# A two-layer graph network on one core: sorted rows laid out for one load per four pairs, tables found part by part, second pass without a loop

## The reference, cut to what matters

```python
# layer 0
agg = segment_sum(x[dst], src)            # row = src, col = dst
agg = agg / (deg[:, None] + 1e-6)
x = layernorm(x + relu(concatenate([x, agg]) @ W + b))
# layer 1 (4 heads of 32)
s = leaky_relu(x_l[src] + x_r[dst] + (edge_attr @ W_e))
alpha = softmax of einsum(s, att) over the edges of each dst
x = layernorm(x + segment_sum(x_l[src] * alpha, dst) + bias)
```

## Time and profile before

| | us |
|---|---|
| median of 3 runs | 1609.33 |
| lowest and highest | 1607.97, 1613.49 |
| the profiled execution | 1610.33 |
| its span, first to last instruction | 1608.5 |
| mean granted TensorE clock | 0.896 of full speed |

### The profile page before, as it was taken

How to read it: one execution, slowest core, us unless ns; L and a number is a source line. 1 busy time by engine, 2 the same in 40 slices (tenths; PEclk the granted TensorE clock), 3 DMA queues, 4 the chain that set the end, 5 groups by cost and what they waited for, 6 DMA issues and landing times. The chain is left out here.

```text
span 1608.5 us, 35020 instructions
## 1 busy us (share of the span) xinstructions
PE 1221.8 (76%) x8692; PEld 1083.7 (67%) x8702; DVE 1002.4 (62%) x2116; ACT 771.1 (48%) x2046; POOL 970.2 (60%) x970
## 2 busy tenths in 40 slices
PE   4887866888887778776797787888878887878650
PEld 2685856877777667765564777777777877777640
DVE  5333324644554444455654588888888878888858
ACT  0375644444455545410144665665655656556311
POOL 3277777777677766740001777777777777777501
PEclk9999889998999998988998899998999989999855
DMA  2233335555555555544101433333333333332001
GB/s 67 73 114 93 105 106 151 140 145 147 144 145 148 150 140 149 149 113 109 40 12 55 134 97 96 95 97 88 95 92 92 96 91 90 87 93 83 26 1 40
DMA packets 235701, 160.30 MB, mean 100 GB/s; under 512 B 29816, under 2 KB 220622, under 8 KB 235580
## 3 DMA queue, kind: packets, MB, share of 16 engines
q1 hardware_dynamic: 206396, 100.85, 24.1%
q0 software_dynamic: 29184, 58.01, 11.9%
HBM read 127.10 MB, written 34.39 MB: 100 GB/s over the span
## 5 line engine op out<-in xcount | busy, mean ns | idle before, releaser
L390 POOL DMA_INDIRECT sorted_rows<-row,place_idx x456 | 468.8, 1028 | 230.8 <-issue 173.5
L1134 POOL DMA_INDIRECT xl<-xl_rows,index_c x456 | 468.8, 1028 | 158.0 <-issue 132.5
L428 ACT COPY onehot_t<-ps_t 128x500 f32<-128x500 f32 x114 | 65.6, 575 | 284.2 <-PE ps_t L735 274.9
L1410 PE MATMUL ps_cs<-w_e,attr_t 128*125 128x128 f32 x912 | 193.9, 298 | 3.7 <-DVE work_c L1324 3.1
L1411 PE MATMUL ps_cs<-src_sum,onehot_ct 128*125 x912 | 191.3, 295 | 0.0
L601 DVE TENSOR_TENSOR away_s<-row_in,pair_bucket 128x4 f32<-128x4 f32 x135 | 21.9, 162 | 223.3 <-DMA row_in<-sorted_rows 215.9
L1410 PEld LDWEIGHTS ps_cs<-w_e,attr_t 128*125 128x125 f32 x912 | 155.4, 213 | 4.2 <-issue 3.3
L746 PE MATMUL ps_g<-row_in,onehot_s 128*128 128x129 f32 x976 | 143.9, 295 | 18.2 <-DVE onehot_s L606 18.2
L1411 PEld LDWEIGHTS ps_cs<-src_sum,onehot_ct 128*125 128x125 f32 x912 | 153.2, 210 | 0.0
L746 PEld LDWEIGHTS ps_g<-row_in,onehot_s 128*128 128x128 f32 x976 | 131.9, 210 | 24.6 <-issue 22.5
L1148 ACT ACTIVATE apart<-column,dst_lo 125x128 f32<-125x128 f32 x456 | 145.6, 394 | 4.6 <-PEq L858 4.6
(11 more groups left out here) (307 smaller groups left out, 2385.8 us busy)
## 6 DMA issues: line engine op xcount, KB each, us to landing
row_in<-sorted_rows SPq DMA_DIRECT2D x540, 66.0 KB
attr<-in_ea SPq DMA_DIRECT2D x456, 62.5 KB
attr_c<-in_ea SPq DMA_DIRECT2D x456, 62.5 KB
sorted_rows<-row,place_idx POOLq DMA_INDIRECT x456
xl<-xl_rows,index_c POOLq DMA_INDIRECT x456, 3.3
xl_rows<-x_nodes SPq DMA_DIRECT2D x5, 320.0 KB, 2.5
out<-x SPq DMA_DIRECT2D x4, 320.0 KB
sorted_rows<-x SPq DMA_DIRECT2D x5, 66.0 KB, 2.0
```

Source lines behind the costliest of these rows:

```text
L390: pool.indirect_dma_start(out=m.sorted_rows.rearrange("k p w -> (k p) w"), out_offset=bass.IndirectOffsetOnAxis(ap=m.place_idx[:, k:k + 1] ...
L1134: pool.indirect_dma_start(out=xl[x][:, u, :], out_offset=None, in_=m.xl_rows, in_offset=bass.IndirectOffsetOnAxis(ap=index[half][:, b * U ...
L1410: pe.matmul(out, attr_t[off % 2][:, u, :], m.w_e[:], start=True, stop=False)
```

## The change

1. `sorted_rows` is laid out as (128, tiles, row) instead of (tiles, 128, row). Four table tiles that follow each other lie side by side in each partition's stretch, so one transfer of 128 x 2112 bytes loads them. `tile2_i` has the first tile of each pair block, and a new table `offset2_i` says which of the four each pair uses; TensorE, VectorE and ScalarE load those numbers.
2. VectorE makes the one-hot matrix of a pair block with four operations of 128 columns, straight from `row_in`. In the last part every second pair block (from 109 on) has it made by ScalarE.
3. `find_ends(p)` finds dst and src of the slots of one part only, in a step of its own; `by_slot` skips the parts of `pick` that are zero. Places are split in two numbers (place mod 128, place / 128). The setup's order changes: places of part 0 come before the number tables.
4. The flags of the softmax move from step 14 to step 78.
5. In `attend` the loop is gone, and POOL reads the indices from `src_idx` itself.

The core of the diff:

```diff
             def load_rows(q):
...
-                tiles = numbers(nc, sp, m.tile2_i, q * U, U, NP * T2 - 1)
-                for u in range(U):
-                    sp.dma_start(row_in[q % B2][:, u, :], m.sorted_rows[bass.ds(tiles[u], 1), :, :].rearrange(
-                        "o p w -> (o p) w")).then_inc(row_back[q % B2], 16)
+                tile = numbers(nc, sp, m.tile2_i, q, 1, NP * T2 - U)[0]
+                sp.dma_start(row_in[q % B2][:], m.sorted_rows[:, bass.ds(tile, U), :]).then_inc(row_back[q % B2], 16)
...
+        def by_scalar(q):
+            return q >= FIRST_ODD and (q - FIRST_ODD) % 2 == 0        # FIRST_ODD = (NP - 1) * G2 + 1
...
+            def make_onehot_s(q):                                      # ScalarE
+                act.wait_ge(row_back[q % B2], 16 * (q // B2 + 1))
...
+                for u in range(U):
+                    act.activation(shift_s[:, u:u + 1], row_in[q % B2][:, bass.ds(offsets[q][u], 1), P + 1], ACT.Identity,
+                                   bias=m.bucket2[:, k:k + 1], scale=-1.0).then_inc(shift_ready, 1)
+                for u in range(U):
+                    act.activation(apart_s[:, u, :], m.column[:], ACT.Abs, bias=shift_s[:, u:u + 1]).then_inc(
+                        apart_s_ready, 1)
+                act.wait_ge(src_summed, q - RINGS + 1)
+                act.activation(onehot_s[q % RINGS][:], apart_s[:], ACT.Relu, bias=1.0, scale=-1.0).then_inc(onehot_s_odd, 1)
...
             def make_onehot_s(q):                                      # VectorE
-                dve.tensor_tensor(away[:], row_in[q % B2][:, :, P + 1], m.bucket2[:, q * U:(q + 1) * U],
-                                  ALU.subtract).then_inc(away_found, 1)
-                dve.tensor_tensor(onehot_s[q % RINGS][:], repeat(m.column[:], 1, U), repeat(away[:], 2, P),
-                                  ALU.is_equal).then_inc(onehot_s_ready, 1)
+                for u in range(U):
+                    src = row_in[q % B2][:, bass.ds(offsets[q][u], 1), P + 1]
+                    dve.scalar_tensor_tensor(onehot_s[q % RINGS][:, u, :], m.column[:], m.bucket2[:, k:k + 1],
+                                             src.broadcast_to([P, P]), ALU.add, ALU.is_equal).then_inc(onehot_s_ready, 1)
...
+            def find_ends(p):                                          # TensorE
+                for at, table in ((0, dst_f), (128, src_f)):
+                    out = ps_c[0:TE, at:at + n]
+                    if p:
+                        pe.matmul(out, table[:, p - 1], pick[:, p - 1, cols], start=True, stop=False)
+                    mm = pe.matmul(out, table[:, p], pick[:, p, cols], start=(p == 0), stop=True)
...
             find_counts(0)
-            by_slot(ps_a[:, 2:4, :].rearrange("p a w -> p (a w)"), TE, dst_f).then_inc(dst_found, 1)
-            turn_starts(0)
+            find_ends(0)
             for c in range(5):
-                if c == 4:
-                    pe.wait_ge(numbers_ready, 1)
+                if c == 3:
+                    pe.wait_ge(dst_ready, 1)
                 sum_chunk(0, c, CHUNK_BANKS[c])
-            count_pairs(0)
-            by_slot(ps_g[:, 2:4, :].rearrange("p a w -> p (a w)"), TE, src_f).then_inc(src_found, 1)
             turn_places(0)
             pick_places(0)
+            turn_starts(0)
+            count_pairs(0)
...
                 for q in gathers(j):                                   # VectorE
-                    make_onehot_s(q)
+                    if not by_scalar(q):
+                        if q % 3 == 0 or q >= FIRST_ODD:
+                            n = 1 if q >= FIRST_ODD - 1 else 3
+                            found = numbers(nc, dve, m.offset2_i, q * U, n * U, U - 1)
...
+                        found = numbers(nc, pe, m.offset2_i, q * U, 3 * U, U - 1)      # TensorE, with window2_i
...
-        FIRST_AT = 14
+        FIRST_AT = 78
...
# attend
-            for j in range(static):
-                one_step(0, j)
-            with engine.Fori(0, LOOPS) as i:
-                for s in range(RING):
-                    one_step(i, static + s)
-            for j in range(static + LOOPS * RING, NB + LAG + 2):
+            for j in range(NB + LAG + 2):
                 one_step(0, j)
...
-                    pool.tensor_copy(index[half][0:TE, :], m.src_idx[:, bass.ds(j * U, GS)]).then_inc(index_ready, 1)
-                    pool.wait_ge(index_ready, i * 2 + off // B + 1)
```

More of the change, by code:

```diff
@@ L453, in _ @@
                         row_copied, 1)
+                if j + 2 < NB:
+                    act.wait_ge(dst_ready, min(((j + 2) * U + U - 1) // CR, NP - 1) + 1)
+                    make_onehot(j + 2)
+                for q in gathers(j):
+                    if by_scalar(q):
+                        act.wait_ge(pairs_ready, NP)
+                        offsets[q] = numbers(nc, act, m.offset2_i, q * U, U, U - 1)
+                        make_onehot_s(q)
                 if (p := phase_at.get((j, "totals"))) is not None:
@@ L557, in _ @@
             link(dve.tensor_tensor(t_of[:], iota_k[0:1, :], node_of[0:1, :], ALU.subtract))
[L558 to L561, removed]
+            find_ends(0)
+            for c in range(5):
+                place_chunk(0, c, CHUNK_BANKS[c])
+            dve.wait_ge(preset, PRESET)
+            place_window(0)
             find_first_pairs(0)
@@ L639, in _ @@
                 if (p := phase_at.get((j, "placed"))) is not None:
+                    find_ends(p)
+                if (p := phase_at.get((j, "stored"))) is not None:
                     place_window(p)
@@ L699, in pick_places, with find_ends @@
                 pe.matmul(out, place_t[:, p % 2, :], pick[:, p, cols], start=(p == 0), stop=True).then_inc(window_found, 1)
-            def by_slot(bank, rows, table):
-                for c in range(CC):
-                    mm = pe.matmul(bank[0:rows, 0:K], table[:, c], pick[:, c, :], start=(c == 0), stop=(c == CC - 1))
+            def find_ends(p):
+                cols = windows[p]
+                n = cols.stop - cols.start
+                if p:
+                    pe.wait_ge(chunk_placed, 5 * (p + 1))
+                for at, table in ((0, dst_f), (128, src_f)):
+                    out = ps_c[0:TE, at:at + n]
+                    if p:
+                        pe.matmul(out, table[:, p - 1], pick[:, p - 1, cols], start=True, stop=False)
+                    mm = pe.matmul(out, table[:, p], pick[:, p, cols], start=(p == 0), stop=True)
+                mm.then_inc(ends_of_slot, 1)
+            def by_slot(bank, rows, table):
+                for p in range(NP):
+                    cols = windows[p]
+                    out = bank[0:rows, cols]
+                    if p:
+                        pe.matmul(out, table[:, p - 1], pick[:, p - 1, cols], start=True, stop=False)
+                    mm = pe.matmul(out, table[:, p], pick[:, p, cols], start=(p == 0), stop=True)
                 return mm
@@ L800, in _ @@
                 if (p := phase_at.get((j, "window"))) is not None:
+                    find_ends(p)
+                if (p := phase_at.get((j, "picked"))) is not None:
                     pick_places(p)
@@ L809, in _ @@
                         pe.wait_ge((first_copied, ends_copied)[which], 1)
-                        for c in range(CC):
-                            mm = pe.matmul(ps_p[0:4, 0:K], ends4[:, which, c, :], pick[:, c, :],
-                                           start=(c == 0), stop=(c == CC - 1))
-                        mm.then_inc(ends_found, 1)
+                        by_slot(ps_p, 4, ends4[:, which]).then_inc(ends_found, 1)
 def center(vec, done, y, stats):
@@ L1032, in attend @@
         xl = [sb(f"xl{b}", [P, U, P]) for b in range(RING)]
-        index = [sb(f"index_c{b}", [P, GS], I32) for b in range(2)]
         onehot = [sb(f"onehot_c{b}", [TE, U, P]) for b in range(RING)]
@@ L1088, in attend, with steps @@
         block = ctx.enter_context(nc.Block())
-        def steps(engine, one_step, static=STATIC):
-            for j in range(static):
-                one_step(0, j)
-            with engine.Fori(0, LOOPS) as i:
-                for s in range(RING):
-                    one_step(i, static + s)
-            for j in range(static + LOOPS * RING, NB + LAG + 2):
+        def steps(engine, one_step):
+            for j in range(NB + LAG + 2):
                 one_step(0, j)
@@ L1115, in _ @@
         def _(pool):
-            for half in range(2):
-                pool.memset(index[half][:], 0).then_inc(index_preset, 1)
-            pool.wait_ge(index_preset, 2)
             def one_step(i, off):
@@ L1452, in one_step @@
                         turned_back, 1)
-            steps(pe, one_step, STATIC - 1)
+            steps(pe, one_step)
 def finish(nc, g, m, out):
```

169 lines of the change are left out of this document (99 added, 70 removed).

## The result

The changed kernel takes 1603.3 us (median of 20 runs, 1595.9 to 1613.7) against 1613.3 us of the kernel before in the same number of runs: a ratio of 0.9941, 95% interval 0.9927 to 0.9954. It is 0.6% faster where 4.5% was forecast, and 1603 lies outside the range of 1505 to 1582. The spans of these two are 1604.5 us after and 1608.5 before: they lie 4 us apart where the medians lie 10 apart. One of the four runs of the experiment with four row loads took 5090 us, and the time given there is the median of the other three.

What follows compares the result with a forecast made beforehand. POOL's floor (5.33 us a block) was taken to bound the first 44 store blocks, SyncE's queue the next 70 and the tail. Savings of 9 + 3 + 24 + 14.5 + 22 = 72.5 us gave 1537 us, range 1518 to 1558.

Steps and rivals of the forecast that it cites:

- the first 44 blocks: First 176 row stores, 237.5 us: POOL's floor sets the pace, 5.40 to 5.33 us a block, 3 us saved.
- Rival 3: Store stage and tail: register loads form a chain that nothing covers, 6.45 us a block, 1651 us in all; chance 0.05.
- SyncE's queue as the bound of the last 70 blocks: Last 280 row stores: one row load for four takes blocks from 5.85 to 5.5 us, 24 us saved.
- My 5.36 for TensorE: Last 70 store blocks: TensorE's sum of 4.86 + 0.3 + 0.2 us a block, taken as 5.5 with VectorE's latency.
- rival 1: Whole kernel: nothing but POOL's floor binds, 104 us saved, 1505 us; chance 0.18.
- The announced sign: Gather stretch: SyncE's queue would wait over a hundred microseconds instead of some 4.
- Rival 2: Register loads take SyncE's place, or issue count costs nothing: store stage stays at 5.85 us a block, 1580 us; chance 0.16.
- Flags at step 78: Softmax flags moved from step 14 to 78: costs nothing if POOL's lead is ten microseconds, 10 us if gone.
- Setup: Before the first store: shorter slot products and a new order bring it from 66.2 to 57 us, 9 us saved.
- Tail: 27 pair blocks after the last store: 2.0 us each instead of 2.54, 54 us in all, 14.5 us saved.
- Rival 4: Tail: row loads are slower as one, 2.6 us a pair block, the tail's gain gone, 1552 us; chance 0.11.
- Second pass: Second pass without loop and index copies: 5.45 us a block instead of 5.65 over 113 blocks, 21 us saved.

Runs made afterwards that it cites:

- the first experiment: The changed kernel with ScalarE's one-hot of block j + 2 again made before the row copy of block j, new wait kept: 1508.0 us, ratio to the kernel before 0.933.
- the kernel with the zeros: The changed kernel with eight matmuls of zeros on TensorE in each of steps 4 to 23: 1585.9 us, ratio 0.9821.

## Why the prediction was wrong

**The step that failed** is in "The change part by part", and it failed by absence: it lists the row load, the flags, the setup and tables, the tail and the second pass, and not the move of ScalarE's one-hot behind the row copy. From it comes "the first 44 blocks go from 5.40 to 5.33: 3 us", which looked only at POOL's floor: they took 6.39. Undoing it gives 5.35. The rows to price it stood in front of me: Abs and Relu take 1.9 us, the row copy 0.58, and TensorE was busy 4.2 us a block in this stretch (184.99 us over 44 blocks): one after the other some 6.7, an estimate from these rows, and not 5.33. Rival 3, "slower", had the right form (a chain that nothing covers, deciding above 6.05 us a block) with the wrong link in it, register loads.

**SyncE's queue as the bound of the last 70 blocks**: right, and sized too small. Without the move these blocks fell by 39 us, not 24 (408.1 to 369.0, 5.27 a block). My 5.36 for TensorE and its 0.14 for VectorE's latency did not bind; rival 1, POOL's floor everywhere, was the better picture. With the move, 7.9 us were lost instead. The announced sign, SyncE's waits over a hundred microseconds, came true in the kernel after, whose queue waited 167.4 us for one releaser in 217 to 650 us:

```profile
SPq L89 <- PE ps_a L847: 167.4, 66, 7.3
```

and the time still didn't come. A queue that is freed shows only that it is no longer the bound, not what is.

**Rival 2, register loads or the number of issues**: the second half is refuted (66 us for the issues). The first did not show at 5.27 us a block. VectorE's wait for row_in, forecast under 40 us, is 0.9 us in the kernel after, whose chain hides it, and 21.7 in the first experiment.

**Flags at step 78**, priced at 0 to 10 us: in the first experiment blocks 80 to 90 take 5.79 us each against 5.16 for the 23 behind them, some 6 us. The trace shows the path. VectorE works on the flags from 492.23 to 497.87 (lines 146 to 163), its add of the attr sum stands behind them, TensorE waits for that add, the row copy for TensorE, and POOL for the row:

```profile
498.10 0.69 DVE L635 TENSOR_TENSOR attr_sum<-attr_sum,ps_a 128x516 f32 x1
498.94 0.59 PE L131 MATMUL ps_a<-zeros 128*128 128x258 bf16 x2 [3.94 <-DVE attr_sum L635]
502.99 0.58 ACT L481 COPY row<-ps_x 125x512 f32<-125x512 f32 x1 [5.56 <-PE ps_x L854]
504.35 0.97 POOL L400 DMA_INDIRECT sorted_rows<-row,place_idx  x1 [4.07 <-issue]
```

No kernel moved them back, so the 6 us are read from the place and from these lines.

**Setup**: 7.3 us instead of 9. The attr loads started at 48.29, forecast 47.5; the first store came at 58.91, forecast 57:

```profile
48.29 11.81 SPq L363 DMA_DIRECT2D attr<-in_ea  x19
58.91 1.16 POOL L400 DMA_INDIRECT sorted_rows<-row,place_idx  x1 [44.93 <-DVE row L662]
```

**Tail**: 51.0 us, forecast 54 for it, 19.2 saved instead of 14.5. 1.9 us a pair block; ScalarE busy 34.75 of 50 us, VectorE 33.06, neither full. The reasons hold: the issues gave most, the split some 6 us. Rival 4, slower row loads, fell with it.

**Second pass**: 28.9 us, forecast 21, with ends of 0 and 32. In the first experiment it is 37.7 us, outside that end. My 5.44 us a block added up loop gaps on VectorE (2.8 us in 12 blocks); taking the loop away brought all of 5.65 down to POOL's 5.31. The kernel after has the same code there and took 9 us longer, and what made that difference stays open. It is not the order on ScalarE: the kernel with the zeros has the order of the kernel after and took 599.1 us. Five executions of this code took 599.1 to 604.8 us, so the 608.4 looks like a matter of the one execution.

**The other 70 blocks of the kernel after** take 5.94 us each, though its clock there is 0.98. Who waited for whom from 340 to 756 us:

```profile
POOL sorted_rows L400 <- issue: 136.5, 264, 5.1
ACT row L478 <- PE ps_x L854: 107.2, 68, 5.4
ACT onehot_t L438 <- PE ps_t L809: 97.7, 68, 4.4
PE ps_t L809 <- ACT onehot L432: 44.1, 39, 1.6
```

The chain is still visible in the last row, and the first experiment shows that all 47 us hang on the order. At this clock a plain step of the chain is no bound: of the 49 steps in which TensorE sums one pair block, the row copies of most are 5.15 us apart. In the 20 steps with two pair blocks the middle value is 6.63 us, because the second sum lies between two links; 20 times 1.48 are some 30 us, an estimate. The flags come on top: blocks 80 to 90 took 61.3 us, against 53.2 in the kernel before with the late one-hot, which has the flags elsewhere. How the rest divides between the tables of the parts and the register loads, no run separated.

With the move undone the stages together give 100 us, where the sum said 72.5: 1508 measured against 1537, below the forecast's own range of 1518 to 1558 and near rival 1's 1505. The signs of the terms were right and the sizes of the two largest too small, 39.1 us for 24 and 37.7 for 21. That the kernel after still came out 0.6% faster, on the side that was forecast, is luck: 55 us of gain and 51.5 of an unseen loss.

## What to carry to other kernels

Read a diff for what changes place, not only for what is added and taken away: a producer moved behind a wait of its own engine turns a pipeline into a chain, and its price is the sum of the links instead of the longest engine. Before pricing the removal of a bound, write down for each engine the order of its loop before and after, and for each item which other engine's next step it feeds. The mark in a profile is a pair of engines that name each other as releasers with about the same idle time each step, while every engine's busy share falls.

## What the runs showed of the hardware

A short regular idle time of TensorE cost twice: 2.5 us of waiting in each step, and 1.66 us more because the matmuls then ran part of the time at the lower clock (granted 0.75 in such a step, 1.00 with the zeros). 160 matmuls of zeros in that idle time bought 15.5 us in 17 blocks; that mends a symptom, and the right order gave 95 in all.

An issue on SyncE's queue costs about the same for a load four times as large: the last of four 66 KB loads took it 0.33 us, one of 264 KB takes

```profile
434.77 0.36 SPq L353 DMA_DIRECT2D row_in<-sorted_rows  x1
```

From the start of one to the start of the next it is 0.54 us (1.94 less 0.33, over three; the prediction's 0.52 is a little low). Three issues less for each of 135 pair blocks are by this some 217 us of that queue, an estimate, of which 61 showed in the two stages that it paced.
